# FFN slot stage and back stage joined by halves of the batches, and attention's x turned by two DMAs

## The reference

```python
x = x + 0.5 * ffn(layernorm(x))
x = x + attention(layernorm(x))
x = x + 0.5 * ffn(layernorm(x))

def attention(x):                      # 16 heads of 16
    q, k, v = split(x @ W_qkv + b_qkv, 3)
    attn = softmax(q @ k.T) / sqrt(256)
    return (attn @ v) @ W_out + b_out

def ffn(x):                            # 64 slots, per batch
    h = gelu([x, mean(slots)] @ w1 + b1)
    alpha = top-8 softmax of (h @ w2 + b2) / (|tau| + 0.1)     # 1024 x 64
    si = alpha.T @ x / alpha.sum(tokens)                       # 64 x 256
    r, z, n = gates of (si @ Wih.T + bih, slots @ Whh.T + bhh) # GRU step
    S = (1 - z) * n + z * slots
    y = layernorm(S + softmax(q k.T / 8) v)                    # over the 64 slots
    return alpha @ (y @ wvp + bvp) @ wo + bo                   # 1024 x 256
```

## Time and profile before

| | us |
|---|---|
| median of 3 executions | 3597.15 |
| profiled execution, own time | 3598.87 |
| its span, first to last instruction | 3597.0 |
| first FFN, slot stage and back stage | 218 to 364 |
| attention, opening | 364 to 470 |
| attention, 16 batches | 470 to 3217 |
| second FFN, slot stage and back stage | 3451 to 3597 |

### The profile page before, as it was taken

How to read it: one execution, slowest core, us unless ns; L and a number is a source line. 1 busy time by engine, 2 the same in 40 slices (tenths; PEclk the granted TensorE clock), 3 DMA queues, 4 the chain that set the end, 5 groups by cost and what they waited for, 6 DMA issues and landing times. The chain is left out here.

```text
span 3597.0 us, 60628 instructions
## 1 busy us (share of the span) xinstructions
PE 3355.8 (93%) x22538; PEld 1186.5 (33%) x22538; DVE 3016.7 (84%) x4480; ACT 2719.7 (76%) x5316; POOL 1041.8 (29%) x899
## 2 busy tenths in 40 slices
PE   6988489999999999999999999999999999966987
PEld 4654222232232323232323232323232323214653
DVE  6865599999999999999999999999999999916855
ACT  5830168888888888888888888888888888865830
POOL 2410423232323232333333332323232322113410
PEclk8999689999999999999999999999999999997999
DMA  4317201121212122121222122212121212113217
GB/s 128 94 72 289 79 25 43 43 56 43 63 43 58 43 55 51 47 61 41 58 49 60 43 62 46 57 43 55 43 55 43 55 32 63 26 43 113 87 72 304
DMA packets 123094, 246.54 MB, mean 69 GB/s; under 512 B 34657, under 2 KB 75425, under 8 KB 108465
## 3 DMA queue, kind: packets, MB, share of 16 engines
q1 hardware_dynamic: 115712, 208.06, 20.7%
q10 hardware_dynamic: 7088, 34.61, 2.3%
HBM read 121.91 MB, written 51.38 MB: 48 GB/s over the span
## 5 line engine op out<-in xcount | busy, mean ns | idle before, releaser
L1357 DVE TENSOR_REDUCE attn_part_max<-attn_ps 128x2 f32<-128x1024 f32 x2048 | 2446.7, 1221 | 246.3 <-PE attn_ps L1497 203.8
L1622 ACT ACTIVATE attn_probs<-attn_ps 128x512 f32<-128x512 f32 x4096 | 2171.8, 600 | 364.2 <-PE attn_ps L1509 364.1
L1509 PE MATMUL attn_ps<-attn_q_rows,attn_k_rows 50*128 50x512 f16 x4096 | 1273.4, 384 | 29.7 <-ACT attn_probs L1622 16.2
L1497 PE MATMUL attn_ps<-attn_k_rows,attn_q_rows 48*128 48x512 f16 x4096 | 1140.4, 388 | 30.7 <-DVE attn_part_max L1357 26.4
L1523 PE MATMUL attn_ps<-attn_probs,attn_v_ones 128*32 128x512 f32 x8192 | 1091.9, 605 | 0.7 <-ACT attn_probs L1622 0.7
L1509 PEld LDWEIGHTS attn_ps<-attn_q_rows,attn_k_rows 50*128 50x128 f16 x4096 | 307.3, 94 | 1325.5 <-ACT attn_probs L1622 1252.5
L1497 PEld LDWEIGHTS attn_ps<-attn_k_rows,attn_q_rows 48*128 48x128 f16 x4096 | 225.5, 94 | 174.4 <-DVE attn_part_max L1357 159.2
L1523 PEld LDWEIGHTS attn_ps<-attn_probs,attn_v_ones 128*32 128x32 f32 x8192 | 161.1, 108 | 237.4 <-issue 136.8
L1449 PE MATMUL attn_ps<-attn_xn_parts,attn_w_qk 128*128 128x256 f16 x1536 | 214.3, 278 | 6.0 <-POOL attn_xn_parts L1281 6.0
L1244 POOL CAST attn_max_parts<-attn_max_whole 32x128 f16<-32x128 f32 x64 | 17.9, 280 | 689.0 <-ACT attn_max_whole L1574 667.8
L1269 POOL TENSOR_TENSOR attn_xn_t<-attn_o_packed,attn_inv_wide 128x1024 f32<-128x1024 f32 x32 | 75.4, 2357 | 397.6 <-DMA attn_inv_wide<-inverse_denominators 397.6
(11 more groups left out here) (172 smaller groups left out, 2600.0 us busy)
## 6 DMA issues: line engine op xcount, KB each, us to landing
attn_q_rows<-attn_parts SPq DMA_DIRECT2D x384, 64.0 KB, 2.3
attn_k_rows<-attn_parts SPq DMA_DIRECT2D x384, 64.0 KB, 2.2
ffn_x_ring<-in_L_attn_x SPq DMA_DIRECT2D x16, 1024.0 KB, 8.3
attn_x_ln<-after_first_ffn SPq DMA_DIRECT2D x16, 1024.0 KB, 4.8
attn_o_packed<-attn_o_sb SPq DMA_DIRECT2D x256, 64.0 KB, 2.3
attn_inv_wide<-inverse_denominators SPq DMA_DIRECT2D x32, 512.0 KB
attn_x_res<-after_first_ffn SPq DMA_DIRECT2D x16, 1024.0 KB, 5.1
after_attention<-attn_x_res SPq DMA_DIRECT2D x16, 1024.0 KB, 8.7
```

The lines of the kernel that those rows point to most:

```text
L1357: dve.tensor_reduce(part_max[:, G % 2, :, j, t, half], pair, AX.X, ALU.max).then_inc(dve_emptied, 1)
L1497: last = pe.matmul(ps[:, bank + e, :], q_rows[rows_e, G % NG, j, t * P:(t + 1) * P], k_rows[rows_e, G % NG, j, half * HALF:(half + 1) * HA ...
L1509: pe.matmul(ps[:, bank, :], k_rows[rows_e, G % NG, h // 2, kt * P:(kt + 1) * P], q_rows[rows_e, G % NG, h // 2, half * HALF:(half + 1) * H ...
L1622: act.activation(probs[:, quad % NQ, h, :], bank_of(s, b0), ACT.Exp, scale=1.0 / (SCALE * SCALE)).then_inc(act_emptied, 1)
```

## The change

It has three parts.

1. **FFN, slot and back stages.** The two stages become one block. All slot work is done in two halves, batches 0 to 7 (h = 0) and 8 to 15 (h = 1), each 512 columns and four PSUM banks, with an order written out by hand that puts steps of one half between steps of the other. `back` of the first half's pairs begins before the second half has been turned. The sigmoid's `* 0.5 + 0.5` instructions are folded into neighbours (gh_t of the candidate is halved in the setup), the zeroing of `attn` goes to GpSimd, the copy of the turned attention to ScalarE.
2. **Back matmuls.** `slot_out` is no longer block-diagonal. A sum is now two token tiles: for each tile two matmuls of 64 rows and 256 columns, the even batch in rows 0 to 63 with one PSUM bank, the odd batch in rows 64 to 127 with the next. One VectorE instruction of 1024 columns adds two tiles. Two pairs of banks take turns. x has a ring of five pairs, and ten batches (10 MiB) are loaded while the slots are computed. Loads and stores are both issued by SyncE.
3. **Attention.** No "turn_x" job is left. GpSimd splits the normalised x before it is turned (`split_x(b0 + 1)` at m = 2, in batch 0 at m = 9 ahead of that quad's `split_max`), and SyncE turns each fp16 part with one DMA transpose of 512 KB (`turn_x`, behind `lay_out` at the end of group 0). The next x is loaded behind them. The quotients are formed in `inv_wide`, so `spread` waits for `ctx_ready`.

```diff
+            RP = 5
+            x_back = sb("x_back", [P, RP, 2, TT, D], F32, own)
...
+                for p in range(RP):
+                    load(p)
+                for p in range(PAIRS):
+                    store(p)
+                    if p >= 1 and p - 1 + RP < PAIRS:
+                        load(p - 1 + RP)
...
+                def back(*numbers):
+                    for n in numbers:
+                        p, i = divmod(n, TILES)
+                        if n % (QP * TILES) == 0:
+                            pe.wait_ge(out_taken[p // QP], QP // 2)
+                        if n >= 2:
+                            pe.wait_ge(added, n - 1)
+                        for t in (2 * i, 2 * i + 1):
+                            for e in range(2):
+                                mine = slice(e * S, (e + 1) * S)
+                                last = pe.matmul(ps[:, 2 * (n % 2) + e, t % 2 * D:(t % 2 + 1) * D], alpha_t[mine, p, t * P:(t + 1) * P],
+                                                 slot_out[mine, p, :], start=True, stop=True)
+                        last.then_inc(mixed, 1)
...
+                def add_back(*numbers):
+                    for n in numbers:
+                        p, i = divmod(n, TILES)
+                        if i == 0:
+                            dve.wait_ge(x_in_place[p], 32)
+                        dve.wait_ge(mixed, n + 1)
+                        here = x_back[:, p % RP, :, 2 * i:2 * i + 2, :].rearrange("p e t d -> p e (t d)")
+                        dve.scalar_tensor_tensor(here, ps[:, 2 * (n % 2):2 * (n % 2) + 2, :], 0.5, here, ALU.mult, ALU.add).then_inc(added, 1)
...
+                take_out(0)
+                add_back(0, 1)
+                y_moments(1)
+                add_back(2, 3)
+                y_normal(1)
+                add_back(*range(4, 12))
+                take_out(1)
+                add_back(*range(12, PAIRS * TILES))
...
-        out += [(17 + f, "turn_x", NX * (b + 1) + f) for f in range(NX)]
...
-    opening = ([("fold", 0)] + [("turn_x", f) for f in range(NX)] + [("qk", i) for i in range(4)] + [("v", i) for i in range(TT)]
+    opening = ([("fold", 0)] + [("qk", i) for i in range(4)] + [("v", i) for i in range(TT)]
...
-        ctx_t = xn_t[:, 0, :]
+        ctx_t = inv_wide
...
+            def turn_x(n):
+
+                if n > 0:
+                    sp.wait_ge(act_filled, act_slot["qk", 4 * NG * n - 1] + 1)
+                for part, made in ((0, xn_high), (1, xn_low)):
+                    sp.wait_ge(made, n + 1)
+                    sp.dma_start_transpose(xn_parts[:, part].rearrange("p t k n -> p (t k) n"),
+                                           x_parts[:, part].rearrange("p t d -> p (t d)")).then_inc(xn_turned, 16)
...
+                    if g == 0 and b0 + 1 < B:
+                        turn_x(b0 + 1)
+                    if g == 0 and b0 + 2 < B:
+                        load_x(b0 + 2)
...
+            def split_x(n):
+
+                pool.wait_ge(xn_ready, n + 1)
+                if n > 0:
+                    pool.wait_ge(xn_turned, 16 * 2 * n)
+                pool.tensor_copy(x_parts[:, 0], x_ln[:, :, :]).then_inc(xn_high, 1)
+                pool.wait_ge(xn_high, n + 1)
+                pool.tensor_tensor(x_parts[:, 1], x_ln[:, :, :], x_parts[:, 0], ALU.subtract).then_inc(xn_low, 1)
...
                     if m == 9 and b0 == 0:
                         rsqrt(0, 0, 1)
                         normalise(0, 0, 1)
+                        split_x(1)
...
+                    if m == 2 and 0 < b0 < B - 1:
+                        split_x(b0 + 1)
```

More of the change, by code:

```diff
@@ new lines, in scores, with slots_again @@
+                def scores(h):
+                    pe.wait_ge(qk_taken[h], 2)
+                    for b in range(HB):
+                        low = b % 2 * S
+                        last = pe.matmul(ps[low:low + S, 4 * h, b // 2 * S:(b // 2 + 1) * S], q_t[:, b * S:(b + 1) * S],
+                                         k_t[:, b * S:(b + 1) * S], start=True, stop=True)
+                    last.then_inc(score_ready[h], 1)
+                def slots_again(h):
+                    for a in range(QP):
+                        if a % 2 == 0:
+                            pe.wait_ge(v_taken[h], a // 2 + 1)
+                        for k in range(KT):
+                            pe.matmul(y[h][a][:, k * P:(k + 1) * P], new_t[:, h, k, a * P:(a + 1) * P], c.ident[:, :],
+                                      start=(a % 2 == 0 and k == 0), stop=False, skip_group_check=True)
@@ new lines, in turn_attn, with attend @@
+                def turn_attn(h):
+                    pe.wait_ge(attn_ready[h], 2)
+                    for a in range(QP):
+                        last = pe.transpose(ps[:, 4 * h + 1, a * P:(a + 1) * P], attn[:, a, :], c.ident[:, :])
+                    last.then_inc(attn_turned[h], 1)
+                def attend(h):
+                    pe.wait_ge(attn_taken[h], 1)
+                    for a in range(QP):
+                        pe.matmul(y[h][a], attn_t[:, a, :], v_sb[h][:, a, :], start=False, stop=True,
+                                  skip_group_check=True).then_inc(y_ready[h], 1)
@@ new lines, in val, with out @@
+                        last.then_inc(val_ready[h], 1)
+                def out(h):
+                    pe.wait_ge(val_taken[h], KT)
+                    for a in range(QP):
+                        for k in range(KT):
+                            last = pe.matmul(ps[:, 4 * h + a // 2, a % 2 * D:(a % 2 + 1) * D], val_t[:, h, k, a * P:(a + 1) * P],
+                                             c.wo[:, k, :], start=(k == 0), stop=(k == KT - 1))
+                        if a % 2:
+                            last.then_inc(out_ready[h], 1)
@@ L719, in _ @@
+                out(0)
+                attend(1)
+                back(0, 1, 2, 3, 4, 5)
+                turn_y(1)
+                back(6, 7)
+                val(1)
+                back(8, 9)
+                out(1)
+                back(*range(10, PAIRS * TILES))
             @block.vector
@@ L1296, in _ @@
             normalise(0, 0, 0)
-            for k in range(KT):
-                split_x(0, 0, 0, k)
+            split_x(0)
             for G in range(PREP):
```

610 lines of the change are left out of this document (267 added, 343 removed).

## The result

The changed kernel takes **3537.57 us** (median of four runs, 3536.24 to 3539.06); the kernel before took 3599.31 beside it (3596.80 to 3604.74). The ratio is 0.983 (95% interval 0.981 to 0.984). The forecast was 3532, and the profiled execution of the change took 3536.24 us by its own time, 62.6 less than 3598.87.

A forecast was written before the change was run, and what follows sets the result against it. No single engine bounds the whole: TensorE the FFN's slot stage, DMAs its back stage, exponentials attention's plain quads. 3598.87 - 29.4 + 3.9 + 5.3 - 44.8 = 3533.9; less 1.7, 3532 us; range 3514 to 3556.

The forecast's parts named there:

- Turn_x jobs gone: Attention, batches 0 to 14: four quads in each lose a job of 0.49 us, 29.4 us less.
- The transposes hide: Attention batches: two transposes of 6.8 us each land in 13.6 us, within 30.4 us of cover, and cost nothing.
- Opening: Attention's opening: the low part's transpose lands at 398.5, where the first projection started at 394.55; 3.9 us more.
- Batch 0: Attention, batch 0: split_x(1) ahead of split_max on GpSimd delays the maxima; all three engines stand for 5.3 us, once.
- FFN up to the first back matmul: Both FFNs: back matmuls begin at T + 55.7 us, T being the start of the first gate product.
- Rival B: FFN: the halves don't cover each other, 10 us of waiting stay instead of 2; 3548 us, chance 0.12.
- A sum of two tiles: FFN back stage: 0.88 us a sum on TensorE with overlapping row halves, 1.28 on VectorE, which leads, ending near T + 107.5.
- DMA: FFN back stage: 16 MiB queued without a gap at 428 GB/s; DMA ends the stage at T + 123.6, 22.4 us less each.
- The 1 us for the shared queue: FFN back stage: 1 us added for stores and loads sharing SyncE's queue, whose loads wait for landings with stores behind them.
- A: FFN back stage: a sum costs 1.76 us on TensorE, by no overlap or a falling clock; 3545 us, chance 0.17.
- C: Attention: transposes miss m = 28, a pair takes 36.8 us, TensorE stands in 15 batches; 3654 us, chance 0.09.

## Why the prediction was right, and where it was off

*Turn_x jobs gone, -29.4.* Right: 172.3 to 170.4 us in batches 1 to 14, and batch 0 without its stall 170.7 to 168.7. That is 1.9 to 2.0 us a batch, 4 x 0.49.

*The transposes hide.* Right in sign and in the cover of 30 us. Their price was off: I took 6.8 us each, and 6.8 to 8.6 us pass until both of a pair have landed. The row that I took it from, a 512 KB broadcast, is no transpose; that 13.6 us for a pair was up to twice what it takes did no harm, because the cover hides either. The Trainium skill's 261 GB/s ("DMA: Bandwidth & Descriptors", "Latency and other measured facts"), which the page gives for a non-contiguous middle dimension, with about 350 to 400 for the contiguous case, made it an estimated 2.0 us each. The trace does not agree: from 1690 to 1696 us, with the pair under way and the DMAs at a share of 1.03, they move 193 GB/s, and a reader of one transpose waits 4.8 us from its issue. The opening got longer, not shorter.

*Opening, +3.9.* 1.3 measured. The first projection started 375.64 - 370.76 = 4.9 us after the low part was ready and not 6.8, which is 1.9 of the 2.6 us. The rest is less than the opening varies by itself: 106.0 to 108.4 us in the nine other traces in which each pair is issued once.

*Batch 0, +5.3.* 6.2 by the run that removes it: the mechanism was the one named, ended by the DMA of the maxima. Quad 15 loses 5.1 us, close to the sum; the 1.1 us of the quad behind it were not in it.

*FFN up to the first back matmul, T + 55.7.* Measured 272.32 - 217.02 = T + 55.3. Rival B, T + 64, is out. Pair 0 was stored from T + 63.1 (T + 64) and pair 2 from T + 81.4 (T + 81).

*A sum of two tiles.* 16 records, two sums, take 2.00 us: 1.0 a sum where I had 0.88 by overlap, and VectorE 1.2 where I had 1.28. VectorE leads, as said; its last add ends at T + 112.3 instead of T + 107.5, of which 3.65 is the wait for pair 7.

*DMA: the step that was mis-sized.* "From then on work is queued without a gap" held nearly: the share is 0.94 to 1.01 from 298 us on, 0.98 in the mean. "16 MiB at 2.45 us (428 GB/s) are 39.2 us" did not: they took 298 to 341.5 us, 43.5 us at a mean of 393 GB/s. A share of 1.01 does not say 428 GB/s: the 428 came from a window of the kernel before, and its window of 306 to 330 us had 404 at a share of 1.00. The 1 us for the shared queue, counted beside it, was about 1.7. Instead of T + 123.6 the stage ended at T + 126.6, 3 us in each FFN. In the profiled execution the sum stood at 3533.9 and the time at 3536.2: 5.9 for the FFNs, less 2.6 for the opening and 1.0 for the rest. That the total came as close as it did is in part luck: the opening's error ran against the FFNs'.

*Rivals.* A did not occur. It was priced too low, though: in the run with one row half the clock fell too, and 3.4 and 1.7 us were all that the FFNs still gained, where A had left 16. B did not occur. C did not occur: a pair of 33 us would have been needed, and four pairs one behind the other stay under it.

## What to carry to other kernels

Where one stage has idle DMAs and the next is nothing but DMA, each MiB that finds room before the full stretch is worth its whole transfer time (here 2.5 to 3.2 us), and dead buffers of the earlier stage are that room. Price a full stretch by the bytes per second that the trace shows for the same mixture of loads, stores and queues, never by the best window with the same busy share. And when a step is moved to an in-order engine, look at what it now stands in front of in the first pass, where the steady state's slack is missing.

## What the runs showed of the hardware

- fp32 matmuls of 64 rows in the two row halves overlap: 1.0 us for four matmuls of 256 columns, 1.8 us on one half.
- In the one execution with one row half at a time the granted clock fell to 0.53 (279 to 301 us) although TensorE was busy 21.4 of 22 us; in pairs, at 20.3 busy, it was 0.92. A busy engine is not by that at its full clock.
- In three traces the granted clock is 0.79 over the first 8 us of an FFN's slot work, with TensorE busy all the 8 us, where the changed kernel has 1.00. It costs 1.7 us each time, and a stage must be compared with that in mind.
- In batch 15 the maxima are over at quad 40, and TensorE has scores and sums alone. In some executions the clock then falls and a quad takes 3.69 us instead of 2.39; that the kernel before has it too is read from its untraced times alone (3618 to 3630 us). The same window, 3115 to 3165 us, in the run with the loads on ScalarE's queue and in the change:

```profile
3115.00:3165.00 50.00, 45.83 (x161) 5.92 (x159) 0.00 (x0) 29.19 (x58) 10.68 (x6) 0.51 0.14 43
```

```profile
3115.00:3165.00 50.00, 39.84 (x251) 8.99 (x251) 0.00 (x0) 43.87 (x87) 10.72 (x6) 1.00 0.16 48
```

  Why it falls in one execution and not in the next, no run here shows; filling TensorE there was not tried.
- Two DMA transposes of 512 KB take 4.2 to 5.6 us to issue one behind the other, and 6.8 to 8.6 us until both have landed; the DMAs move 193 GB/s meanwhile (1690 to 1696 us), at a share of 1.03.
- Loads that stand between stores on one queue: 340 GB/s from 302 to 310 us at a share of 1.01, and 417 at 1.00 with the loads on another queue.
